# QR stage of a conditioned transformer block: side work dealt anew among the steps, and unread 512-column matmuls on TensorE

## What is computed

```python
U, _ = qr(P)                                 # P: 288 x 64
v = silu(cond) @ W.T + b                     # 2016 entries for each of 2 batches
A[:, iu, ju] = v; A[:, ju, iu] = -v          # 64 x 64, skew-symmetric
z = x @ U                                    # all tokens, onto 64 directions
x = x + (z @ expm(A) - z) @ U.T
# then, with ada = silu(cond) @ ada_w + ada_b split in six:
x = x + gate_msa * attention(modulate(layernorm(x), shift_msa, scale_msa))
x = x + gate_mlp * mlp(modulate(layernorm(x), shift_mlp, scale_mlp))
```

## Time and profile before

| | |
|---|---|
| median of 3 runs | 496.74 us (494.12 to 499.04) |
| the profiled execution | 497.95 us, of which the span in the profile is 496.1 us |
| PE, busy share | 87% (4501 matmul records) |
| weight loads on PE | 58% |
| DVE | 57% |
| ACT | 47% |
| POOL | 18% |
| mean granted TensorE clock, by the profile's records | 0.955 of full speed |

### The profile page before, as it was taken

One profiled execution on the slowest core, in us unless ns is written; L12 is line 12 of the kernel. 1 busy time (PEld: TensorE's weight loads), 2 busy tenths in 40 slices (PEclk: granted clock), 3 DMA queues, 4 the chain that ended last, 5 costly groups with the idle time before them and its releaser, 6 DMA issues.

```text
span 496.1 us, 11092 instructions
## 1 busy us (share of the span) xinstructions
PE 433.6 (87%) x4501; PEld 289.3 (58%) x4501; DVE 280.6 (57%) x787; ACT 233.1 (47%) x479; POOL 89.0 (18%) x108
## 2 busy tenths in 40 slices
PE   5999979998958999899977788778759999999997
PEld 3766655777345666566645565556524456475675
DVE  3598753567466555666746622136887873735522
ACT  3245423242034888687776787842246520602100
POOL 5079999810000000000000000003510000000000
PEclk9999999999997999899979888889969999999999
DMA  6993000000000000000000000000000001000011
GB/s 182 325 311 103 1 4 1 2 2 1 1 0 1 1 1 3 1 3 3 1 5 5 3 4 1 3 1 2 1 1 0 1 12 37 1 24 25 13 48 38
DMA packets 7783, 14.53 MB, mean 29 GB/s; under 512 B 2540, under 2 KB 6097, under 8 KB 7606
## 3 DMA queue, kind: packets, MB, share of 16 engines
q1 hardware_dynamic: 7732, 13.82, 9.1%
HBM read 11.37 MB, written 2.38 MB: 28 GB/s over the span
## 4 chain that ended last, share of the span: by engine, by line
PE 66%; DVE 15%; ACT 11%; issue 7%; DMA 0%; SPq 0%; DVEq 0%; ACTq 0%
PE psum L852 12%; PE psum L870 11%; PE psum L712 6%; PE psum L552 3%; PE psum L784 3%; PE psum L508 3%; PE psum L556 3%; ACT scratch L965 2%; PE psum L637 2%; PE psum L564 2%; DVE MX L1240 2%; PE psum L698 2%; PE psum L798 2%; PE psum L499 2%; ACT big L997 2%
## 5 line engine op out<-in xcount | busy, mean ns | idle before, releaser
L852 PE MATMUL psum<-scratch,W 128*128 128x512 f16 (+1 forms) x252 | 58.2, 392 | 2.3 <-DVE scratch L1235 2.3
L454 POOL TENSOR_TENSOR X<-X,big 128x288 f32<-128x288 f32 x16 | 12.5, 791 | 249.6 <-DVE big L1339 248.4
L870 PE MATMUL psum<-W,big 128*128 128x288 f16 x432 | 55.7, 286 | 0.0
L712 PE MATMUL psum<-WQ,scratch 128*128 128x288 f16 (+1 forms) x336 | 51.1, 296 | 5.2 <-DVE scratch L1246 5.2
L870 PEld LDWEIGHTS psum<-W,big 128*128 128x128 f16 x432 | 41.0, 98 | 13.7 <-issue 3.8
L1075 ACT ACTIVATE big<-psum 128x512 f32<-128x512 f32 x36 | 21.6, 599 | 57.9 <-PE psum L852 56.9
L1240 DVE TENSOR_REDUCE MX<-psum 128x8 f32<-128x1024 f32 x32 | 39.1, 1221 | 14.8 <-PE psum L662 14.2
L852 PEld LDWEIGHTS psum<-scratch,W 128*128 128x128 f16 (+1 forms) x252 | 25.2, 100 | 33.4 <-issue 3.6
L965 ACT ACTIVATE scratch<-psum,MOD 128x512 f32<-128x512 f32 (+3 forms) x48 | 33.6, 774 | 21.2 <-PE psum L637 7.8
L712 PEld LDWEIGHTS psum<-WQ,scratch 128*128 128x128 f16 (+1 forms) x336 | 31.1, 101 | 17.5 <-issue 6.4
L1019 ACT ACTIVATE big<-psum 128x1024 f32<-128x1024 f32 x32 | 33.2, 1036 | 16.1 <-PE psum L747 15.8
(11 more groups left out here) (200 smaller groups left out, 834.5 us busy)
## 6 DMA issues: line engine op xcount, KB each, us to landing
X<-in_x_dram SPq DMA_DIRECT2D x4, 576.0 KB, 15.0
out_dram<-big SPq DMA_DIRECT2D x16, 144.0 KB, 1.7
big<-in_L_cond_W_dram SPq DMA_DIRECT2D x1, 2268.0 KB
big<-in_L_cond_ada_w_dram SPq DMA_DIRECT2D x2, 864.0 KB, 16.4
stage<-in_L_cond_fc_w_dram SPq DMA_DIRECT2D x1, 1296.0 KB
big<-in_L_cond_fc_w_dram SPq DMA_DIRECT2D x1, 1152.0 KB
stage<-in_L_cond_qkv_w_dram SPq DMA_DIRECT2D x1, 864.0 KB
big<-in_L_cond_fc_w_dram SPq DMA_DIRECT2D x3, 144.0 KB
```

The lines of the kernel that those rows point to most:

```text
L712: mm = pe.matmul(UB[gu % 2][:, 0:D], HT[0:r, n % 2, a_, P * a:P * a + P], WQ[0:r, w_, D * w:D * w + D], start=(p_ == 0), stop=(p_ == 6))
L852: mm = pe.matmul(FB[idx % 3], W1[0:r, w_, P * m:P * m + P], HT[0:r, n % 2, a_, :], start=(p_ == 0), stop=(p_ == 6))
L870: mm = pe.matmul(YB[t % 2][:, 0:D], g[:, a_, f, cols], W2[:, w_, f, :], start=False, stop=(f == NF - 1 and w_ == 1))
```

## The change

It changes the QR stage in four ways.

- **Unread matmuls.** A new function `clock` issues a float32 matmul of a 128 x 128 weight block over 512 columns (one column of an SBUF tile, repeated) into a PSUM bank that nobody reads at that time. Six stand ahead of the Gram matrix, behind a memset that DVE does first (semaphore `dense`); one stands ahead of step 0, and one in each step k = 0 to 63, behind L564 and ahead of the exponential's matmuls and the fillers.
- **Fillers.** "ada 0" moves ahead of (0,3); each of its 4 pieces has a step of its own. The projections (0,3) and (1,3) have 6 pieces of 256 columns where they had 12 of 128, again one in a step. The other pieces go two to a step to the end. All are done at k = 51 where it was 53.
- **Entries v.** They start at k = 7, two in each of five steps and then one; V_END is 33, EXP_AT is 44.
- **The bias.** Its DMA is issued ahead of the one for W on SP's queue; PE copies it into PSUM (one small matmul at k = 6), and the sum at V_END reads it from there, where it read SBUF.

```diff
...
         in_wq, in_wp, in_w1, in_w2 = (sem(n) for n in ("in_wq", "in_wp", "in_w1", "in_w2"))
         in_x = [sem(f"in_x{i}") for i in range(NCH)]
         consts = sem("consts")
+        dense = sem("dense")
         pool_step = sem("pool_step")
         ct_clear = sem("ct_clear")
         silu_e = sem("silu_e")
...
         MISC = bank[7]
         TWOP, BELOW, IIP, ROTP = MISC[R:P, 0:R], MISC[:, 2 * R:3 * R + 2], bank[2][:, 0:2 * R], bank[5]
         UPPER, LOWER = slice(0, R), slice(R, P)
+        BRP = SPREAD[1][0:WROWS, D:D + WTILES]
         work = ["P'", (0, 0), (0, 1), (0, 2), (2, 0), (2, 1), (2, 2), (1, 0), (1, 1), (1, 2), (3, 0), (3, 1), (3, 2),
-                (0, 3), "ada 0", (1, 3), "mod"]
+                "ada 0", (0, 3), (1, 3), "mod"]
         ADA_ROWS = ((0, 1, 3, 4), (2, 5))
         FG = len(work)
         work.append("ada 1")
...
         XDONE = [work.index((i + 2, 2)) + 1 for i in range(2)]
         pieces = []
         for n, w in enumerate(work[:FG]):
-            pieces += [(n, p_) for p_ in range({"P'": 6, "mod": 3}.get(w, 4 if w[0] == "a" else 12 if w[1] == 3 else 4))]
+            pieces += [(n, p_) for p_ in range({"P'": 6, "mod": 3}.get(w, 4 if w[0] == "a" else 6 if w[1] == 3 else 4))]
         last_piece = {n: i for i, (n, _) in enumerate(pieces)}
         ROWS_AT = 4
+        PRELUDE = 6
         LAG = 2
-        EXP_AT = 43
+        EXP_AT = 44
         piece_at, k, room = [], 7, 2
-        for _ in pieces:
+        for n, _ in pieces:
+            alone = work[n] == "ada 0" or work[n] in ((0, 3), (1, 3))
+            if alone and room == 1:
+                k += 1
             piece_at.append(k)
             room -= 1
-            if not room:
-                k, room = k + 1, 2 if k + 1 < EXP_AT + 2 else 1
+            if alone or not room:
+                k, room = k + 1, 2
         def skew_now(k):
-            n = B * (k - 8) if k < 16 else 16 + k - 16
-            return range(n, min(n + (2 if k < 16 else 1), B * WTILES)) if k >= 8 else range(0)
-        V_END = 32
+            n = B * (k - 7) if k < 12 else 5 + k - 7
+            return range(n, min(n + (2 if k < 12 else 1), B * WTILES)) if k >= 7 else range(0)
+        V_END = 33
         NEXP = 3 + SQUARINGS
         LAST = max(piece_at[-1] + 3, EXP_AT + NEXP + 3, R + 1)
-        assert sum(len(skew_now(k)) for k in range(V_END)) == B * WTILES
+        assert sum(len(skew_now(k)) for k in range(V_END + 1)) == B * WTILES
+        assert all(piece_at[last_piece[work.index((i, 3))]] >= V_END for i in range(2))
         TURN1_AT = 4
...
             sp.wait_ge(ct_clear, 1)
             for b, (r0, n) in enumerate(BLK):
                 sp.dma_start(CT[0:n, b, :], c[:, r0:r0 + n].rearrange("b p -> p b"), allow_slow_non_contiguous=True).then_inc(in_c, 16)
+            sp.dma_start(BR, bskew.rearrange("(p t) -> p t", p=WROWS)).then_inc(in_br, 16)
             sp.dma_start(WL, wskew.rearrange("(p t) n -> p t n", p=WROWS)).then_inc(in_w, 16)
             for i in (0, 2, 1, 3):
                 b, a = divmod(TPC * i, 8)
                 sp.dma_start(X[:, TPC * i:TPC * i + TPC, :], x[b].rearrange("(p a) d -> p a d", a=8)[:, a:a + TPC, :]).then_inc(in_x[i], 16)
-            sp.dma_start(BR, bskew.rearrange("(p t) -> p t", p=WROWS)).then_inc(in_br, 16)
             def staged(w, bias, dst, s_):
                 sp.dma_start(dst[:, 0:2, :], w[0:2 * P, :].rearrange("(b p) n -> p b n", p=P)).then_inc(s_, 16)
...
         @block.tensor
         def _(pe):
+            def clock(out, left):
+                pe.matmul(out[:, 0:CH], left, left[:, 0:1].broadcast_to([P, CH]), start=True, stop=True)
+            pe.wait_ge(dense, 1)
+            for _ in range(PRELUDE):
+                clock(FILL[1], XX[:, :])
             pe.wait_ge(in_p, 48)
             for b, (r0, n) in enumerate(BLK):
                 mm = pe.matmul(EXPM[0:R, 0:R], PS[0:n, b, :], PS[0:n, b, :], start=(b == 0), stop=(b == 2))
...
             pe.wait_ge(consts, 1)
             pe.matmul(TWOP, ident[0:R, 0:R], TWO, start=True, stop=True)
             pe.matmul(BELOW, ident[:, :], below[:, :], start=True, stop=True).then_inc(two_ready, 1)
+            clock(FILL[1], XX[:, :])
             def filler(n, p_):
...
                     q, b = divmod(p_, 3)
                     r0, k = BLK[b]
                     for h in range(2):
-                        c0 = CH * (i + 2 * h) + P * q
-                        mm = pe.matmul(f[R * h:R * h + R, P * q:P * (q + 1)], PS[0:k, b, :],
-                                       XT[0:k, b, c0:c0 + P], start=(b == 0), stop=(b == 2))
+                        c0 = CH * (i + 2 * h) + 2 * P * q
+                        mm = pe.matmul(f[R * h:R * h + R, 2 * P * q:2 * P * (q + 1)], PS[0:k, b, :],
+                                       XT[0:k, b, c0:c0 + 2 * P], start=(b == 0), stop=(b == 2))
                 if (n, p_) == (FG, 3) or n < FG and pieces[last_piece[n]] == (n, p_):
                     mm.then_inc(fill_ready, 1)
...
                     pe.wait_ge(a_sign, j + 1)
                     pe.matmul(out, SG[LOWER, j:j + 1].broadcast_to([R, R]), GA[LOWER, k:R + k + 1],
                               start=False, stop=True).then_inc(a_row, 1)
+                if k < R:
+                    clock(EXPM if k < EXP_AT else SPREAD[1], ident[:, :])
                 if 0 <= k - EXP_AT - 2 < NEXP:
                     exp_step(k - EXP_AT - 2)
                 for i, (n, p_) in enumerate(pieces):
...
                         r0, n = BLK[kb]
                         mm = pe.matmul(SPREAD[b][:, r0:r0 + n], SC32[0:n, kb, b:b + 1].broadcast_to([n, P]), ident[0:n, 0:n],
                                        start=True, stop=True)
+                        if i == 5:
+                            pe.wait_ge(in_br, 16)
+                            mm = pe.matmul(BRP, ident[0:WROWS, 0:WROWS], BR, start=True, stop=True)
                         if kb == 2:
                             mm.then_inc(row_psum, 1)
                 if k == EXP_AT:
...
         @block.vector
         def _(dve):
+            dve.memset(XX[:, :], 1.0).then_inc(dense, 1)
             dve.wait_ge(consts, 1)
             dve.wait_ge(in_p, 48)
             dve.tensor_copy(GA[LOWER, LAG:R + LAG], PS[0:R, 0, :]).then_inc(new, 1)
...
                 skew_entries(k)
                 if k == V_END:
                     dve.wait_ge(v_sum, B * WTILES)
-                    dve.wait_ge(in_br, 16)
-                    dve.tensor_tensor(VR[:, 1], VR[:, 0], BR.unsqueeze(1).broadcast_to([WROWS, B, WTILES]), ALU.add).then_inc(v_all, 1)
+                    dve.tensor_tensor(VR[:, 1], VR[:, 0], BRP.unsqueeze(1).broadcast_to([WROWS, B, WTILES]), ALU.add).then_inc(v_all, 1)
                 if -1 <= k - EXP_AT - 2 < NEXP:
                     exp_out(k - EXP_AT - 2)
                 if k == R - 1:
```

## The result

The changed kernel takes 503.76 us (median of 4 runs, 503.18 to 505.94), beside 497.31 (494.12 to 499.04) for the kernel before on the same chip: 1.0145 times as long, 95% interval 1.0084 to 1.0206. It is slower by 1.4%.

A forecast was written before the change was run, and what follows sets the result against it. PE was taken to bound every QR step at the raised clock. Start +5.3, loop +7.0 and behind the loop -2.5 gave +9.8 us on the span, 496.74 to 506.5 us; range 496 to 515, 499 to 514 for this case.

The forecast's parts named there:

- The case forecast: Whole kernel: PE bound in every QR step, +9.8 us on the span, 506.5 us; chance 0.66.
- The clock: PE runs the QR stage at 1.2 GHz; dense wide matmuls double the pace after 4.0 us and hold it through the loop.
- The price of the wide matmul: One unread 512-column matmul in a step: two passes, first load and shape changes on both sides, 1.16 us.
- The first rival: A wide matmul costs half, 0.43 us, as its moving operand is one repeated column; 480 us; chance 0.12.
- The third rival: Changes of shape overlap with the wide matmul and the clock holds past the loop; step 1.41, 497.5 us; chance 0.18.
- The bare step: QR step without fillers: PE needs 0.39 us for its own matmuls plus 1.16 for the wide one, 1.55.
- The ring: Chain of PE and three DVE instructions in a QR step: 1.60 us before, 1.41 at the fast clock.
- The sum of the loop: L1146 of k = 0 to that of k = 63: 123.3 us against 116.2 before, +7.0.
- The start: Six slow wide matmuls ahead of Gram end at 8.3 us; L556 at 10.8 where it was 5.49, +5.3.
- Behind the loop: From the loop's end to L637: faster passes of L490, bias passes, L603 and L617 save 2.5 us.
- The rest is as before: X products paced by DVE, clock expected to fall there, L637 slow again; no change in time counted.
- The second: Clock doesn't rise or falls back inside the loop: bare step 2.83 us, about 615 us; chance 0.04.

The follow-up runs named there:

- the kernel with the prelude alone: The changed kernel with the six unread matmuls ahead of the Gram matrix and none behind them: 494.5 us, ratio 0.9967 to the kernel before.
- the second one: The changed kernel with a second unread 512-column matmul behind the first in each of the 64 steps: 561.71 us, ratio 1.1306 to the kernel before.
- the deal: The changed kernel without any unread matmuls, only side work dealt anew and the bias in PSUM: 491.43 us, ratio 0.989 to the kernel before.

## Why the prediction was right

The case forecast is the one that happened, at 503.8 us against 506.5: slower by more than 1%. The mechanism and its price a step are borne out. That the totals are so near is in part luck: from span to span +9.8 us was forecast and +5.4 measured, and of the 4.4 between them the choice of the base, 496.74 in place of the profiled 497.95, took back 1.2; the median after also lies 0.4 above its profiled execution. The 4.4 are 0.7 at the start, 1.4 in the loop, 2.6 behind L637, less 0.3 between. By its own steps:

**The clock.** That the QR stage runs at 1.2 GHz under a row of nines was right, and the kernel with the prelude alone shows it by a record. That the six matmuls raise it was right; the time from their start was 3.2 us (1.12 to about 4.3, from the passes' starts) and not 4.0. That it holds to the end of the loop and falls in the X products, L657 staying slow, was right. The holding was the weakest step: it was argued from the 0.85 us of wide matmul in a step, with no row for such a mix, and the runs with 192 and 128 columns show that it could have gone the other way with a narrower one.

**The price of the wide matmul.** 1.16 us was forecast for a step; 1.06 from its start to the next matmul and 0.10 ahead of it were measured, and 0.86 for the second one, which is the streaming alone. The first rival (half price) is out, and so is the third's condition, that the changes of shape overlap with it.

**The bare step.** 1.55 was forecast and 1.55 measured (14.88 to 16.43), a light step with two transposes 1.77 and 1.77. The ring of 1.41 shows where PE is taken off it: 1.42.

**The sum of the loop.** 123.3 was forecast, 121.8 measured:

| steps | forecast | measured |
|---|---|---|
| k = 0 to 3 | 5.9 | 6.04 |
| 4 to 6 | 6.7 | 6.71 |
| 7 to 9 | 6.5 | 6.41 |
| 10 to 33 | 43.5 | 42.39 |
| 34 to 37 | 8.6 | 8.67 |
| 38 to 43 | 12.8 | 12.76 |
| 44 and 45 | 5.2 | 4.73 |
| 46 to 49 | 9.7 | 10.02 |
| 50 and 51 | 4.3 | 4.43 |
| 52 to 62 | 20.1 | 19.65 |

In k = 34 to 53 the prediction's words and its sum do not agree: by its words the heavy steps gain a little, by its sum they take 44.3 us where they took 41.2. The sum was right, 44.18. The 1.1 us in k = 10 to 33 are one mis-sized term: the transposes of the third block (L514, a 128 x 32 weight block) were costed at 0.35 for two further changes of shape. PE in time there:
```profile
48.97 1.13 PE L467 MATMUL psum<-ident 128*128 128x512 f32 x2
49.94 0.38 PE L514 MATMUL psum<-ident,X 128*32 128x128 f32 x2
50.25 0.27 PE L567 MATMUL psum<-scratch,ident 64*64 64x65 f32 x1
```
L514 starts 0.97 us behind L467 where a 64 x 64 block starts 1.06 behind: to a block of the same 128 rows there was no change to pay, 0.09 less, and it takes 0.31 to the next. These 8 steps took 1.77 like the others, not 1.90. Another 0.45 lies in k = 52 to 62: a step with an exponential alone was summed at 1.83 and took 1.79, since the next step's own matmuls follow a block of their own shape: the two passes of L571 start 0.06 us apart there (131.75 and 131.81), 0.10 in a bare step (15.95 and 16.05).

**The bias.** 0.3 us and hidden was forecast; the sum takes 0.19 us at 71.8, again under an instruction of POOL, and in the kernel with the bias alone the loop gains 2.9 us.

**The start.** +5.3 was forecast, +4.6 measured (L1146 of k = 0 from 6.44 to 11.02). The Gram matrix starts at 8.05 and not at 8.3, as the clock rose sooner; from there to the first L571 it is 2.17 and not 2.45; and from that to the first update 0.80, where it was 0.95 before and no saving was counted.

**Behind the loop.** -2.5 was forecast for the way to L637, -2.2 measured (10.2 late at k = 63, 8.0 late at L637). Its first term failed: L592 (now L612) was to start 0.8 sooner and starts 0.26 sooner, 9.92 late, because ACT's L954 comes 0.5 later behind k = 63 than L934 did. One unread matmul stands in that step too, ahead of the exponential's last products; that this is the reason was not tried. The products between gained a little more than forecast, 2.0 against 1.75.

**The rest is as before: wrong by 2.6 us.** Of the 8.0 us at L637 5.4 are left at the end of the profile. From the first projection on (L712, now L732) both kernels run the same instructions; PE alone, of before and then of after, with its clock:
```profile
151.27:496.10 344.83, 302.92 (x3552) 0.94 0.03 9
```
```profile
158.94:501.50 342.56, 300.58 (x3552) 0.95 0.03 9
```
The same 3552 matmuls take 2.3 us less under a clock that is slightly higher. The kernel with 256 columns takes 345.7 us for them, and over all thirteen profiles they take 342.5 to 345.7, so this is hardly an effect of the change's own; the executions of the kernel before alone lie 5 us apart. It could not have been forecast, only allowed for.

**The third rival** named what would have been needed: a step no longer than the ring. It did not come for free, since the changes of shape are paid; the 256 columns bring it by streaming less. The second, with the clock lost inside the loop, is what 128 columns did.

## What to carry to other kernels

Price unread work on TensorE like any other work: two full passes of its columns in float32 and a change of array shape on both sides, against the slack that the ring leaves at the raised clock. Here the slack was 1.41 - 0.39 = 1.02 us less the fillers, 512 columns cost 1.16 and 256 columns 0.73 (an estimate: 1.16 less the 0.43 of streaming), and this alone made +1.4% of one and -2.4% of the other. Read the clock from the pace of one known matmul at two places before believing a clock row, and judge each part of a change by itself: here the deal's 5 us of gain were hidden under 12 us of unread matmuls, 3 of them for the prelude and 9 for those from step 0 on.

## What was not expected of the hardware

- The clock can stay low while PE always has a matmul in flight: it stood at half for 13.6 us in which PE was busy for 13.6, in the kernel without unread matmuls in k = 34 to 51. It had fallen behind 6.2 us with PE busy for 5.9.
- Raising the clock and holding it are two questions. The prelude raised it in each profile; what stood in the steps decided whether it stayed: in the profiles 256 and 512 columns held it through the loop, 192 lost it in the heavy steps, 128 lost it at k = 3, and with none it was lost within the first two steps.
- With less of it the same program gives different times: 478 to 507 us with 192 columns, 480 to 499 with 256 and no prelude, 477 to 488 without it in k = 34 to 51, while 256 with a prelude of three stays within 2.2 us in four executions.
- The clock also rose by itself for short spells in the loop of kernels without unread matmuls there (66.9 to 70.4 us in one profile, 97.2 to 104.0 in another), and a comparison of two single profiles can be off by such a spell, 1.4 us here.
- A change from a 128 x 128 block to a 128 x 32 block cost nothing measurable, to a 64 x 64 block 0.10 us.
